# Pyramid-pooled attention: the last batch convolved in two rounds, exp and probabilities in PSUM, x split on GpSimd

## The reference

```python
qk = relu(bn(conv1x1(x, qk_w)))            # 256 channels
val = relu(bn(conv1x1(x, v_w)))            # 512 channels
key = psp(qk)                              # adaptive max pools 1, 3, 6, 8: 110 cells
value = psp(val).transpose(0, 2, 1)
query = qk.reshape(B, 256, 4096).transpose(0, 2, 1)
p = softmax(einsum('bnc,bcs->bns', query, key) * 256 ** -0.5)
y = einsum('bns,bsc->bnc', p, value)
return x + bn(conv1x1(y, out_w))           # y back as channels by pixels
```

## Time and profile before

| | |
|---|---|
| median of 3 runs | 1428.84 us (1428.83 to 1429.14) |
| the profiled execution | 1426.75 us, span 1424.9 us |
| PE busy | 1387.3 us (97%), 6029 matmuls and transposes |
| DVE busy | 917.8 us (64%) |
| ACT busy | 474.8 us (33%) |
| POOL busy | 240.2 us (17%) |
| HBM | 136.86 MB read, 67.11 MB written, 143 GB/s over the span |
| mean granted clock of PE | 0.992 |

### The profile page before, as it was taken

How to read it: one execution, slowest core, us unless ns; L and a number is a source line. 1 busy time by engine, 2 the same in 40 slices (tenths; PEclk the granted TensorE clock), 3 DMA queues, 4 the chain that set the end, 5 groups by cost and what they waited for, 6 DMA issues and landing times.

```text
span 1424.9 us, 15729 instructions
## 1 busy us (share of the span) xinstructions
PE 1387.3 (97%) x6029; PEld 1134.4 (80%) x6029; DVE 917.8 (64%) x1745; ACT 474.8 (33%) x662; POOL 240.2 (17%) x141
## 2 busy tenths in 40 slices
PE   7999999999999999999999999999999999999776
PEld 6888888888888888888888888888888888888654
DVE  6555656657656666657656767656766657656678
ACT  4112333333333333333333333333333332333243
POOL 0000121121121121121121121221121221221252
PEclk9999999999999999999999999999999999999989
DMA  5112234534434534434434534434524434434456
GB/s 192 60 59 90 88 118 148 178 120 146 171 125 148 177 112 155 173 122 148 162 132 150 177 119 148 167 128 148 177 106 161 169 127 148 156 132 156 142 196 223
DMA packets 102941, 204.98 MB, mean 144 GB/s; under 512 B 3243, under 2 KB 3283, under 8 KB 102867
## 3 DMA queue, kind: packets, MB, share of 16 engines
q1 hardware_dynamic: 102290, 202.93, 40.5%
q10 hardware_dynamic: 576, 1.05, 0.2%
HBM read 136.86 MB, written 67.11 MB: 143 GB/s over the span
## 4 chain that ended last, share of the span: by engine, by line
PE 95%; DVE 3%; issue 1%; ACT 1%; DMA 0%; SPq 0%
PE conv_ps L330 25%; PE conv_ps L328 25%; PE conv_ps L329 24%; PE out_ps L367 4%; PE out_ps L368 4%; PE out_ps L369 4%; PE score_ps L342 2%; PE score_ps L343 2%; PE score_ps L344 2%; PE sum_ps L354 1%; PE sum_ps L353 1%; PE sum_ps L379 0%; PE sum_ps L381 0%; PE sum_ps L380 0%; DVE e_l L696 0%
## 5 line engine op out<-in xcount | busy, mean ns | idle before, releaser
L328 PE MATMUL conv_ps<-xh,wh 128*128 128x512 f32 x1536 | 602.2, 392 | 0.0
L330 PE MATMUL conv_ps<-xl,wh 128*128 128x512 f32 x1536 | 601.6, 392 | 0.0
L329 PE MATMUL conv_ps<-xh,wl 128*128 128x512 f32 x1536 | 598.5, 390 | 0.0
L623 DVE TENSOR_REDUCE row_max<-conv_ps 128x64 f32<-128x512 f32 (+2 forms) x576 | 289.1, 530 | 441.5 <-ACT q L471 370.8
L330 PEld LDWEIGHTS conv_ps<-xl,wh 128*128 128x128 f32 x1536 | 288.6, 188 | 63.9
L329 PEld LDWEIGHTS conv_ps<-xh,wl 128*128 128x128 f32 x1536 | 288.9, 188 | 63.2
L328 PEld LDWEIGHTS conv_ps<-xh,wh 128*128 128x128 f32 x1536 | 288.8, 188 | 61.3
L273 POOL TENSOR_TENSOR e_l<-e,e_h 128x512 fp32r<-128x512 f32 x64 | 83.5, 1305 | 1024.7 <-ACT e_h L485 1024.7
L482 ACT ACTIVATE e<-score_ps 128x512 f32<-128x512 f32 x60 | 35.8, 597 | 488.7 <-PE score_ps L344 488.7
L471 ACT ACTIVATE q<-conv_ps,shift 128x512 f32<-128x512 f32 x128 | 88.2, 689 | 305.0 <-PE conv_ps L330 305.0
L277 POOL TENSOR_TENSOR q_l<-q,q_h 128x1024 fp32r<-128x1024 f32 x64 | 157.9, 2466 | 141.8 <-ACT q_h L477 141.7
(11 more groups left out here) (117 smaller groups left out, 907.7 us busy)
## 6 DMA issues: line engine op xcount, KB each, us to landing
xa<-x SPq DMA_DIRECT2D x65, 1024.0 KB, 7.5
xo<-x SPq DMA_DIRECT2D x58, 1024.0 KB, 5.2
out<-xo SPq DMA_DIRECT2D x58, 1024.0 KB, 4.2
q<-x SPq DMA_DIRECT2D x4, 1024.0 KB, 5.3
out<-q SPq DMA_DIRECT2D x3, 1024.0 KB, 8.7
out<-xa SPq DMA_DIRECT2D x2, 1024.0 KB, 4.2
q<-v_w ACTq DMA_DIRECT2D x4, 256.0 KB, 4.3
xa<-x SPq DMA_DIRECT2D x2, 512.0 KB, 5.6
```

Of the source, the lines that this page charges most:

```text
L328: nc.tensor.matmul(bank(s, c)[:, :], wh[:, k, cols], hi, start=(k == 0), stop=False)
L329: nc.tensor.matmul(bank(s, c)[:, :], wl[:, k, cols], hi, start=False, stop=False)
L330: last = nc.tensor.matmul(bank(s, c)[:, :], wh[:, k, cols], lo, start=False, stop=(k == KC - 1))
L623: last = nc.vector.tensor_reduce(row_max[:, c, n, :], src[:, r0_ * W:r1_ * W].rearrange("p (r w) -> p w r", w=W), AX.X, ALU.max)
```

## The change

The steps become X = 72. Steps 0 to 55 convolve all six channel groups as before. **Round one**, steps 56 to 63, convolves only the queries' channels (4, 5) of the last batch, while batch 6 goes through attention. **Round two**, steps 64 to 71, loads the same eight tiles of x a second time and convolves the values' channels (0 to 3), while the last batch's own scores, exps and probabilities are made. After step 71 only the last values, one tile's probabilities and all 32 projections of the last batch are left (`make_last_values`, `last_values_hi` and `last_values_lo` work in four slices of 128 columns). Convolutions use three banks from step 56 on, and the fourth becomes a second bank of scores.

Exp, sums and probabilities are kept in PSUM: `exps` writes into its scores' bank, `normalise` multiplies it there and `refine` works in the sums' bank. e and s_r0 are gone from SBUF, and e_h and e_l grow to six tiles, so that the last batch's probabilities can wait for their values. DVE's low half of e (`split_e_lo`) now reads PSUM. POOL takes over both halves of x's low part (except for tile 0) ahead of q's in each step. The diff, cut to its core:

```diff
+    LAST = S - NT
+    X = S + NT
...
-        e = sb("e", [ROWS, 3, TN])
-        e_h = sb("e_h", [ROWS, 3, TN], F32R)
-        e_l = sb("e_l", [ROWS, 3, TN], F32R)
+        e_h = sb("e_h", [ROWS, 6, TN], F32R)
+        e_l = sb("e_l", [ROWS, 6, TN], F32R)
...
+        def channels(s):
+            return range(CC) if s < LAST else range(VC, CC) if s < S else range(VC)
+        def group(s, c):
+            if s < LAST:
+                return CC * s + c
+            if s < S:
+                return CC * LAST + QC * (s - LAST) + c - VC
+            return CC * LAST + QC * NT + VC * (s - S) + c
...
         def bank(s, c):
-            return conv_ps[(CC * s + c) % 4]
+            g = group(s, c)
+            return conv_ps[g % 4] if s < LAST else conv_ps[(g - CC * LAST) % 3]
         def score_bank(a):
-            return conv_ps[0] if a >= LAST and a % 2 else score_ps
+            return conv_ps[3] if a >= LAST - NT and a % 2 else score_ps
         def pv_bank(k):
-            return conv_ps[1] if k == B - 1 else sum_ps
+            return out_ps[1] if k == B - 1 else sum_ps
         def out_bank(a, m):
-            return [*out_ps, conv_ps[2], conv_ps[3]][m] if a >= LAST - 1 else out_ps[m % 2]
+            return [out_ps[0], *conv_ps[0:3]][m] if a >= LAST else out_ps[m % 2]
...
+        def e_slot(a):
+            if a < S - 2:
+                return e_h[:, a % 6, :], e_l[:, a % 6, :]
+            qq = [q_h, q_l][a - (S - 2)]
+            return qq[:, 1, 0, :], qq[:, 1, 1, :]
...
+                if s + 2 < X:
+                    sp.wait_ge(x_lo, 2 * s + 2)
+                    load(s + 2)
+                if s - NT - 2 < LAST:
+                    if s > LAST:
+                        store(s - NT - 2)
+                    stored(s - NT - 2)
+                    load_residual(s - NT)
...
-            def split_e_lo(a):
-                pool.wait_ge(e_hi, a + 1)
-                wait(pool, out_done, OC * (a - 2))
-                u = a % 3
-                nc.gpsimd.tensor_tensor(e_l[:, u, :], e[:, u, :], e_h[:, u, :], ALU.subtract).then_inc(e_lo, 1)
+            def split_lo(s, part):
+                pool.wait_ge(x_hi, 2 * s + part + 1)
+                ks = slice(part * HALF, (part + 1) * HALF)
+                nc.gpsimd.tensor_tensor(xl[:, s % 2, ks, :], xa[:, s % 2, ks, :], xh[:, s % 2, ks, :], ALU.subtract)\
+                    .then_inc(x_lo, 1)
...
-            for s in range(S):
-                if s >= NT:
-                    split_e_lo(s - NT)
-                if s >= NT - 1:
+            pool.wait_ge(x_lo, 2)
+            for s in range(X):
+                if s + 1 < X:
+                    split_lo(s + 1, 0)
+                    split_lo(s + 1, 1)
+                if NT - 1 <= s < X - 1:
                     split_q_lo(s - (NT - 1))
...
                     pe.wait_ge(key_ready, a // NT + 1)
                 pe.wait_ge(q_lo, a + 1)
-                wait(pe, exp_done, a - 1 if a > LAST else a)
-                if a == LAST + 1:
-                    pe.wait_ge(rows_pooled, CC * S)
-                sc, u = score_bank(a)[0:ROWS, :], a % 2
+                wait(pe, p_lo, a - 1 if a > LAST - NT else a)
+                if a == LAST - NT + 1:
+                    pe.wait_ge(rows_pooled, CC * LAST)
...
+                if a == LAST:
+                    pe.wait_ge(vo_lo, B + m)
+                    wait(pe, rows_pooled, GROUPS)
+                elif m == 0 and a % NT == 0:
+                    pe.wait_ge(vo_lo, a // NT + 1)
+                wait(pe, out_added, OC * a + m - (3 if a > LAST else 1))
...
+            for s in range(LAST, S):
+                ap, ac = s - NT - 1, s - NT
+                sums(ap)
+                if s == LAST:
+                    conv(s, 4)
+                scores(ac)
+                if s > LAST + 1:
+                    project(ap - 1, 2)
+                    project(ap - 1, 3)
+                if s > LAST:
+                    conv(s, 4)
+                conv(s, 5)
+                project(ap, 0)
+                project(ap, 1)
+                if s == LAST:
+                    for m in range(VC):
+                        project_values(ac // NT, m)
+                    project(ap, 2)
+                    project(ap, 3)
+            for s in range(S, X):
+                ap, ac = s - NT - 1, s - NT
+                sums(ap)
+                if s == S:
+                    project(ap - 1, 2)
+                    project(ap - 1, 3)
+                conv(s, 0)
+                conv(s, 1)
+                if s == S:
+                    project(ap, 0)
+                    project(ap, 1)
+                scores(ac)
+                conv(s, 2)
+                if s == S:
+                    project(ap, 2)
+                    project(ap, 3)
+                conv(s, 3)
+            for m in range(VC - 1):
+                project_values(B - 1, m)
+            sums(S - 1)
+            project_values(B - 1, VC - 1)
...
             def exps(a):
                 act.wait_ge(scores_done, a + 1)
-                wait(act, p_lo, a - 2)
-                nc.scalar.activation(e[:, a % 3, :], score_bank(a)[0:ROWS, :], ACT.Exp).then_inc(exp_done, 1)
+                sc = score_bank(a)
+                nc.scalar.activation(sc[:, :], sc[:, :], ACT.Exp).then_inc(exp_done, 1)
                 act.wait_ge(exp_done, a + 1)
-                wait(act, out_done, OC * (a - 2))
-                nc.scalar.activation(e_h[:, a % 3, :], e[:, a % 3, :], ACT.Copy).then_inc(e_hi, 1)
+                if a < S - 2:
+                    wait(act, out_done, OC * (a - 5))
+                nc.scalar.activation(e_slot(a)[0], sc[:, :], ACT.Copy).then_inc(e_hi, 1)
...
                     guess(ap)
-                if s + 1 < S:
+                if LAST < s < S:
+                    exps(ac)
+                if s + 1 < X:
                     split_hi(s + 1, 0)
                 if ap >= 0:
                     split_p_hi(ap)
-                if s + 1 < S:
+                if s + 1 < X:
                     split_hi(s + 1, 1)
-                if ac >= 0:
+                if ac >= 0 and not LAST < s < S:
                     exps(ac)
-                if ac + 1 >= 0:
+                if 0 <= ac + 1 < S:
                     split_q_hi(ac + 1)
-                store_q(s, 0)
-                if ac >= 0 and ac % NT == 0:
-                    values_hi(ac // NT)
-                store_q(s, 1)
...
-                nc.vector.scalar_tensor_tensor(s_r0[:, :], sum_ps[0:ROWS, :], -1.0, r0[:, :], ALU.mult, ALU.mult)\
+                nc.vector.scalar_tensor_tensor(sum_ps[:, :], sum_ps[:, :], -1.0, r0[:, :], ALU.mult, ALU.mult)\
...
-                nc.vector.tensor_tensor(e[:, u, :], e[:, u, :], rsum[:, :], ALU.mult).then_inc(p_made, 1)
+                sc = score_bank(a)
+                nc.vector.tensor_tensor(sc[:, :], sc[:, :], rsum[:, :], ALU.mult).then_inc(p_made, 1)
+            def split_e_lo(a):
+                dve.wait_ge(e_hi, a + 1)
+                hi, lo = e_slot(a)
+                nc.vector.tensor_tensor(lo, score_bank(a)[:, :], hi, ALU.subtract).then_inc(e_lo, 1)
             def split_p_lo(a):
                 dve.wait_ge(p_hi, a + 1)
-                u = a % 3
-                nc.vector.tensor_tensor(e_l[:, u, :], e[:, u, :], e_h[:, u, :], ALU.subtract).then_inc(p_lo, 1)
+                hi, lo = e_slot(a)
+                nc.vector.tensor_tensor(lo, score_bank(a)[:, :], hi, ALU.subtract).then_inc(p_lo, 1)
...
-                if s + 1 < S:
-                    split_lo(s + 1, 0)
...
+                if ac >= 0:
+                    split_e_lo(ac)
...
+            for s in range(LAST, S):
+                ap, ac = s - NT - 1, s - NT
+                refine(ap)
+                normalise(ap)
+                if s == LAST + 1:
+                    values_lo(ap // NT)
+                if s == LAST:
+                    pool_cells(s - 1, 0, CC)
+                    split_p_lo(ap)
+                    finish_grids(s, 0, CC)
+                    finish_keys()
+                    finish_values(0, VC)
+                    pool_rows(s, 4)
+                    split_e_lo(ac)
+                else:
+                    split_e_lo(ac)
+                    if s > LAST + 1:
+                        add_out(ap - 1, 2)
+                    split_p_lo(ap)
+                    if s > LAST + 1:
+                        add_out(ap - 1, 3)
+                    pool_cells(s - 1, VC, CC)
+                    pool_rows(s, 4)
+                pool_rows(s, 5)
+                add_out(ap, 0)
+                add_out(ap, 1)
+                if s == LAST:
+                    make_values(ac // NT)
+                    add_out(ap, 2)
+                    add_out(ap, 3)
+            for s in range(S, X):
+                ap, ac = s - NT - 1, s - NT
+                refine(ap)
+                normalise(ap)
+                if s == S:
+                    add_out(ap - 1, 2)
+                    add_out(ap - 1, 3)
```

(25 more changed lines are left out.)

318 lines of the change are left out of this document (142 added, 176 removed).

## The result

| | before | after |
|---|---|---|
| median | 1428.87 us (5 runs, 1428.83 to 1429.27) | 1423.04 us (5 runs, 1422.37 to 1424.11) |
| ratio to before, 95% interval | | 0.9965 [0.9952, 0.9977] |
| the profiled execution | 1426.75 us, span 1424.9 us | 1424.07 us, span 1422.4 us |
| DVE / POOL busy | 917.8 / 240.2 us | 847.2 / 498.1 us |
| PE busy | 1387.3 us | 1386.1 us |

It is 5.8 us faster (forecast 9.4).

A forecast was written before the change was run, and what follows sets the result against it. PE was taken to bound the kernel, with 38.3 us idle or slow after step 56's start. Terms 22.3 + 76.4 + 19.3 + 89.8 + 35.0 = 242.8 against 252.2 gave 9.4 us less, median 1419.4; range 1408 to 1430.

The forecast's parts named there:

- Steps up to 55, nothing: Tile steps before round one: the moved DVE and POOL work hides, 1.8 us to spare in the tightest place.
- Step 56, 22.3: Round one's first step: 12.8 us of matmuls, 7.7 waiting for keys after a DVE/POOL collision, 1.8 of slow matmuls.
- Steps 57 to 63, 76.4: Rest of round one: six 11.06 us loops through ACT and POOL set the pace; 7.2 us are waits.
- What moving x onto POOL could cost, nothing: DVE beside POOL: large loop operations except values_lo have PSUM and SBUF inputs, costed at their old times.
- The third rival: SBUF port: every DVE operation waits for POOL, 37 us more, 1456 us; chance 0.04.
- Writing results back into PSUM, free: DVE and ACT results written to PSUM: taken as no extra cost; upper bound 0.6 us on each operation.
- Step 64, 19.3: Round two's first step: 16.95 us for 74 matmuls plus a 2.3 us wait for the last batch's keys.
- steps 65 to 71, 89.8: Rest of round two: 56 matmuls, 12.8 us each, with no wait.
- The end, 35.0: After the last convolution: 34.7 us by PE's chain, 34.0 plus a landing by the stores, taken as 35.0.
- the first: Rival: round one's loop is not closed, so no waits there, 7.2 us less, 1412.2; chance 0.10.
- the second: Rival: POOL at its slowest, 2.89 us, and a second key-chain collision, 1430.3, no difference; chance 0.10.
- the fourth: Rival: DMA limits round one, its loads and store in series, 35 us more, 1454; chance 0.08.

The follow-up runs named there:

- e10: The changed kernel itself, unedited, timed and profiled a second time: 1422.91 us, span 1420.8.
- e2: Against the changed kernel, ACT does x's first half ahead of exp in steps 57 to 63: 1415.46 us, ratio to the kernel before 0.9914.
- e6: Against the kernel before, only x's low halves moved to POOL, with exp and probabilities in SBUF and one round: 1524.66 us in one execution.
- e3: Against the changed kernel, the last batch's stores issued in quarters, each behind its own addition: 1421.14 us, ratio to the kernel before 0.9951.
- c2: Against the changed kernel, six single edits combined (stores by quarters, PE kept busy, exp reordered among them), with further step 56 moves: 1405.44 us, ratio to before 0.9842.
- e4: Against the changed kernel, 8 and 5 unread matmuls fill PE's two gaps ahead of the last projections: 1421.41 us, ratio to the kernel before 0.9956.
- e5: Against the changed kernel, x's low halves made on DVE again in every step, POOL keeping only q's: 1430.50 us, ratio to the kernel before 1.0020.

## Why the prediction was right, and where it was off

The direction, the mechanism and the places held; the gain was forecast 3.6 us too large in the medians. By its own steps, on the profiled execution:

- **Steps up to 55, nothing:** right, no gap.
- **Step 56, 22.3:** measured 22.9. The collision came, on the second grid operation as forecast, with the keys 10.7 us in (10.9). The slow clock behind cost 2.5 us on 12 matmuls, not 1.8 on nine. In e10 the step took 22.6.
- **Steps 57 to 63, 76.4:** measured 77.2, the loop 11.14 us for 11.06. e2 shows that it was this loop: the 6 us went with it. But "each wait is near 1 us, too short for the slow clock" fails for the first one: step 57 has six matmuls fewer, so its wait was 2.54 us, as the prediction's own loop implies (11.06 less 8.7). In e10 slow matmuls followed it, and most of what they cost fell into the next wait.
- **What moving x onto POOL could cost, nothing:** right for all operations with PSUM in them (684 ns for 681). The third rival had every DVE operation wait for POOL. Only those with two SBUF inputs did, and in e6, where the product is one of them, the time is 97 us more. The Trainium skill's advice (Perfetto Trace Analysis, Optimizing Scalar/DVE Operations), that moving work between the two might not help, fits e6 and not the change. The rule that separates them stands in the Trainium skill as well (SBUF — State Buffer, Who interferes with whom): a DVE instruction with at most one SBUF input, outside DVE's 2-port modes, does not contend with GpSimd, and one with two SBUF inputs contends with a GpSimd instruction that reads SBUF. The traces agree, 0.70 against 2.77 us.
- **Writing results back into PSUM, free:** right, 0.70 us on DVE (L746, L736), against 0.69 for the earlier trace rows's `refine`.
- **Step 64, 19.3 and steps 65 to 71, 89.8:** measured 19.1 and 89.6. The wait was 1.3, not 2.3, and 0.28 was lost at an addition.
- **The end, 35.0: this step failed,** measured 40.1, and in the second profile 39.1. It is 5.1 of the 6.1 us by which the sum came out short: 0.4 until the first projection, 2.0 in the projections, 3.0 behind the last addition, less the 0.3 by which 34.7 was rounded up. Two terms were mis-sized. The **3.1 us behind the last addition** was taken over from a kernel whose last projections came at gaps; here PE makes 1 MiB in 2.75 us, as fast as the stores take it away (2.76 at 380 GB/s), so what the stores lose at the start is still owed at the end, 6.1. The prediction had divided 8 MiB by 372 GB/s from a first store at 11.4 us on. The first store came at 13.6, and the windows up to 1405 moved 213 and 264 GB/s. Stores of whole tiles are 1.8 us of it (e3); why it doesn't fall to 3.1 even with quarters (4.2, and 3.8 in c2) stays open. And the **clock**: the prediction had no term for slow matmuls here, though it forecast two short gaps around the last value product. The nine matmuls from 1390.41 to 1394.32 took 3.9 us instead of 2.06, 1.9 more, and the three ahead of them were slow as well. e4, with PE kept busy, won only 1.0 to 1.2 on the projections, since PE then lost 0.45 us to a wait for an addition.
- **Profiled execution and median:** 1417.4 was forecast for the profiled execution, and it took 1424.07, 6.7 more. I carried over that it lies 2.1 us below the median; it lay 1.0 above, which takes 3.1 off the miss in the median: 3.6. That the median came out nearer than the profiled execution is luck: no step of the prediction accounts for it.

Of the rivals, the first (no loop) was wrong for this kernel and came true by e2's edit; the second needs POOL at 2.89 us in every step, and it ran at 2.36 to 2.49, but for one pair in step 57 that took 5.16 us (4.77 otherwise); the fourth needs PE to wait for x, and no such wait is in the trace. In one 11 us window of round one the DMA engines' share was 0.82 (columns of the earlier trace rows):

```profile
1218.00:1229.00 11.00, 10.20 (x45) 8.08 (x44) 8.21 (x20) 7.00 (x10) 7.00 (x4) 1.00 0.82 286
```

Step 56 starts 0.8 us later than before in the first profile and not in the second (1172.70). These 0.8 us lie ahead of all tile steps: the last wait of the preparation of the weights ends at 34.44 us there, at 33.65 before and at 33.66 in e10.

No part works alone. The rounds and the PSUM tiles without POOL's x are 2.9 us slower than before (e5), x on POOL without them 97 us (e6), together they are 5.8 faster. The rounds alone and the PSUM tiles alone were not run.

## What to carry to other kernels

Before moving work from DVE to GpSimd, sort DVE's operations that will run beside it by how many inputs they have in SBUF: those with one in PSUM kept their time here, those with two waited for the end of a GpSimd operation that had started first. Look for the loop that an order closes (scores, exp, x, POOL, scores): moving x's first half ahead of exp on ACT was worth as much again as the whole change (6.0 us in the steps' times, 7.6 in the medians). And cost a tail whose producer and stores run at the same rate from the first store's start, with the clock that short gaps leave.
